# A layer-norm's statistics and its gate products moved between the bodies of a fused Mamba and MoE kernel

## The reference, cut to what matters

```python
x = x + tanh(g_xattn) * ssm(ctx, z=layernorm(x))        # ssm: conv, scan over 16 states, y * silu(z)
x = x + tanh(g_ffn)   * moe(layernorm(x))               # moe: softmax routing, 8 experts with adapters, shared expert

def _layernorm(x, axis=-1, eps=1e-05):
    m = jnp.mean(x, axis=axis, keepdims=True)
    v = jnp.var(x, axis=axis, keepdims=True)
    return (x - m) / jnp.sqrt(v + eps)
# in the ssm: y = y * jax.nn.silu(z), z the layer norm of x
```

## Time and profile before

| what | value |
|---|---|
| median of three runs | 1623.14 us (1621.38 to 1624.61) |
| profiled execution, its own time | 1615.96 us |
| its span | 1614.1 us |
| TensorE busy | 1509.3 us (94%) |
| VectorE busy | 1160.2 us (72%) |
| GpSimd busy | 743.1 us (46%) |
| ScalarE busy | 659.8 us (41%) |
| granted TensorE clock, mean | 0.978 |

### The profile page before, as it was taken

How to read it: one execution, slowest core, us unless ns; L and a number is a source line. 1 busy time by engine, 2 the same in 40 slices (tenths; PEclk the granted TensorE clock), 3 DMA queues, 4 the chain that set the end, 5 groups by cost and what they waited for, 6 DMA issues and landing times.

```text
span 1614.1 us, 19148 instructions
## 1 busy us (share of the span) xinstructions
PE 1509.3 (94%) x6440; PEld 1146.2 (71%) x6440; DVE 1160.2 (72%) x1638; ACT 659.8 (41%) x1035; POOL 743.1 (46%) x536
## 2 busy tenths in 40 slices
PE   5678799988888899999999999999999999999999
PEld 3334377766666667778777777777777777887787
DVE  6899867988899867688888856888888653333333
ACT  6555345544454434543444345434444321211111
POOL 3589421887878702287777401676777000000000
PEclk9799899998999999999999999999999999999999
DMA  7799538698878873889789645899897458778882
GB/s 257 260 334 313 208 114 273 212 317 291 280 269 286 282 257 143 246 294 296 249 254 276 230 150 200 261 301 276 265 283 231 172 191 261 223 220 247 252 244 97
DMA packets 144945, 395.99 MB, mean 245 GB/s; under 512 B 25456, under 2 KB 66672, under 8 KB 129616
## 3 DMA queue, kind: packets, MB, share of 16 engines
q1 hardware_dynamic: 124624, 342.07, 63.5%
q10 hardware_dynamic: 20224, 52.70, 11.3%
HBM read 306.30 MB, written 68.16 MB: 232 GB/s over the span
## 4 chain that ended last, share of the span: by engine, by line
PE 59%; DVE 17%; POOL 9%; issue 5%; ACT 5%; DMA 4%; ACTq 1%; SPq 1%; DVEq 0%; POOLq 0%
PE b_u L819 14%; PE b_g L819 14%; PE b_u L913 8%; POOL ring L1516 5%; PE b_q L913 4%; PE b_q L867 3%; DVE ring L1613 3%; PE b_g L913 3%; PE b_g L885 3%; DVE tt L1587 2%; DMA raw<-in_gu 2%; PE b_g L852 2%; PE b_u L852 2%; DVE ring L1619 2%; POOL gm L1461 2%
## 5 line engine op out<-in xcount | busy, mean ns | idle before, releaser
L1516 POOL TENSOR_TENSOR ring<-du,rep 128x512 f32<-128x512 f32 x256 | 348.5, 1369 | 136.8 <-DVE du L1695 106.3
L819 PE MATMUL b_g<-xnb,gm 128*128 128x512 f32 (+1 forms) x1440 | 352.6, 394 | 0.9 <-DVE xnb L1590 0.9
L819 PE MATMUL b_u<-xnb,gm 128*128 128x512 f32 (+1 forms) x1440 | 349.4, 392 | 0.8 <-DVE xx L1587 0.8
L1525 POOL TENSOR_TENSOR yx<-yx,ring 128x512 f32<-128x512 f32 x192 | 266.2, 1387 | 152.1 <-DVE ring L1619 151.5
L1613 DVE TENSOR_TENSOR_SCAN ring<-b_a,ring 128x512 f32<-128x512 f32 x256 | 310.8, 1214 | 16.0 <-ACT b_a L1060 14.3
L819 PEld LDWEIGHTS b_g<-xnb,gm 128*128 128x128 f32 (+1 forms) x1440 | 256.0, 179 | 78.9 <-issue 8.8
L819 PEld LDWEIGHTS b_u<-xnb,gm 128*128 128x128 f32 (+1 forms) x1440 | 257.4, 179 | 73.1 <-DVE xx L1587 2.0
L1587 DVE SCALAR_TENSOR_TENSOR tt<-tt,b_g 128x512 f32<-128x512 f32 (+1 forms) x120 | 82.0, 684 | 197.4 <-ACT tt L1060 197.2
L1060 ACT ACTIVATE b_a<-delta,cs 128x512 f32<-128x512 f32 x256 | 173.3, 681 | 80.0 <-DVE ring L1613 75.8
L913 PE MATMUL b_u<-dwt,hhl 128*128 128x512 f32 (+1 forms) x720 | 193.7, 399 | 3.0 <-DVE daw_s L1590 1.7
L1060 ACT ACTIVATE tt<-b_g 128x512 f32<-128x512 f32 (+1 forms) x120 | 71.2, 593 | 284.4 <-PE b_u L852 241.2
(11 more groups left out here) (248 smaller groups left out, 1923.9 us busy)
## 6 DMA issues: line engine op xcount, KB each, us to landing
gm<-scr_gm SPq DMA_DIRECT2D x64, 1024.0 KB, 9.3
dwt<-scr_dw SPq DMA_DIRECT2D x32, 1536.0 KB, 6.7
rep<-bc_d ACTq DMA_DIRECT2D x64, 512.0 KB, 7.0
gm<-scr_gm SPq DMA_DIRECT2D x32, 768.0 KB, 5.4
scr_gm<-gm SPq DMA_DIRECT2D x20, 1024.0 KB, 7.2
dqt<-scr_dq SPq DMA_DIRECT2D x25, 640.0 KB, 9.1
qat<-scr_qa SPq DMA_DIRECT2D x25, 512.0 KB, 9.2
awt<-aw_h ACTq DMA_DIRECT2D x48, 256.0 KB, 4.7
```

Source lines behind the costliest of these rows:

```text
L819: i = mm(out_b[0:IW[m], :], w, v, start=(n == 0), stop=(n == 11 and not is_routed(s)))
L1516: v.tensor_tensor(ring_at(nb, T), du[:, T % 4, :], rep[:, N % NREP, 0], ALU.mult).then_inc(pool_dbu, 1)
L1525: v.tensor_tensor(yd, yd, ring[:, T % NRING], ALU.add).then_inc(pool_y, 1)
```

## The change

On ScalarE the root moves from slot "b" of body 3 to its end, behind slot "f". On VectorE the row sums and the variances move to the end of body 3, behind slot "f" too, and the scales to body 4, in front of slot "b". The four tanh and gate products, two each in bodies 4 and 5, become one in body 4, two in body 5, and one in body 6. No instruction is added or taken away, and no transfer is touched.

```diff
@@ def tanh_z(nb, c), ScalarE
-                need(act, dve_daw, NF * (nb - 1) + (4 if c < 2 else 5))
+                need(act, dve_daw, NF * (nb - 1) + (4, 5, 5, 6)[c])
@@ def routed(b, e), ScalarE
                 slot("b")
                 if split_next:
                     hi("gm0", s + 1)
-                if more and e == 3:
-                    root(2 * nb)
                 if more and e == 4:
                     norm_z(nb, range(LC))
                     tanh_z(nb, 0)
                 if more and e == 5:
-                    tanh_z(nb, 2)
+                    tanh_z(nb, 1)
+                if more and e == 6:
+                    tanh_z(nb, 3)
                 tanh(s, 1)
                 slot("h1")
                 h_hi(s, 1)
-                if more and e == 4:
-                    tanh_z(nb, 1)
                 if more and e == 5:
-                    tanh_z(nb, 3)
+                    tanh_z(nb, 2)
...
                 slot("f")
+                if more and e == 3:
+                    root(2 * nb)
@@ def routed(b, e), VectorE
-                if more and e == 3:
-                    dve.wait_ge(dma_x, 16 * (nb + 1))
-                    for c in range(LC):
-                        row_sums(2 * nb, xx[nb % 2], c)
-                    variances(2 * nb)
+                if more and e == 4:
                     scales(2 * nb, True)
                 slot("b")
...
                 if more and e == 4:
                     gate_z(nb, 0)
                 if more and e == 5:
-                    gate_z(nb, 2)
+                    gate_z(nb, 1)
+                if more and e == 6:
+                    gate_z(nb, 3)
...
                 hidden(s, 1, mid("h1"))
                 slot("c")
-                if more and e == 4:
-                    gate_z(nb, 1)
                 if more and e == 5:
-                    gate_z(nb, 3)
+                    gate_z(nb, 2)
...
                 slot("f")
+                if more and e == 3:
+                    dve.wait_ge(dma_x, 16 * (nb + 1))
+                    for c in range(LC):
+                        row_sums(2 * nb, xx[nb % 2], c)
+                    variances(2 * nb)
```

## The result

The changed kernel takes 1627.36 us (median of 20 runs, 1624.15 to 1632.67), the kernel before 1621.20 (20 runs on the same chips, 1615.03 to 1624.61). The ratio is 1.0042, 95% interval [1.0031, 1.0053]: slower by 6 to 7 us (6.2 between the medians), where -0.5 was forecast, with -4 and +4 as bounds.

The account below looks back on a forecast made before the run. TensorE was taken to bound passes 1 and 2, VectorE pass 0. Pass 0 at -1.3 us and passes 1 and 2 together at +0.8 summed to -0.5: median 1622.6 us, range -4 to +4.

Parts of the forecast that it names:

- the term of the scales: Body 4: six instructions, 1.2 us, delay the normalizations 1.64 us; +0.9 us in each of passes 1 and 2, +0.6 in pass 0.
- The 0.7 that a gate product fewer gives back: Body 4: gate product 1 leaves, giving back about 0.7 us of the delay behind the scales.
- The block at the end of body 3: Seam to body 4: of 3.1 us of statistics 1.95 come to light; body 3 35.45 us, -0.5 in passes 1 and 2 each.
- Rival 2: End of body 3: the statistics are hidden whole, faster, total -7 us, 1616; chance 0.18, in part or whole.
- Pass 0: Body 3: third hidden tile begins by 418.8, body 4 1.9 us earlier (bounds -3.2 and 0); with scales +0.6, sum -1.3 us.
- TensorE's wait at the seam: Pass 0, end of body 3: TensorE waits some 2.6 us for VectorE's first addition in body 4.
- Rival 1: Seams before body 4: TensorE's clock falls behind the wait, 1.3 to 1.7 us each, total +4, 1627; chance 0.20, body 4's upper bound included.
- Root: ScalarE, behind the last exponential of body 3: cost 0; uncovered, 1.3 us a table load.
- gate: Body 5 holds two products as before, body 6 gets one of 0.68 to 2.47 us: cost 0; uncovered, up to 1.1 in pass 0.
- rival 3: Only moved: body 3's lateness reappears whole, half at the seam, half in body 4; no difference, 1623.1; chance 0.17.
- one of the prediction's signs of being wrong: A body 6 that grew; others were a seam without a wait, or a clock under 1.00 behind it in passes 1 and 2.

Follow-up runs that it names:

- with GpSimd held: The changed kernel, with GpSimd's step behind the first hidden tile of body 4 waiting until the next batch's scales are done: 1622.81 us, ratio to before 1.0016.
- The double block: The changed kernel with scales at the head of body 4 and the four row sums at the end of body 3 done twice: 1631.12 us, ratio to before 1.0058.
- spread version: The changed kernel with scales at the head of body 4 and row sums spread over bodies 2 and 3 (pass 0: within body 3): 1611.11 us, ratio to before 0.9943.
- the version with the scales at the head: The changed kernel with the six scale instructions moved to the head of body 4, behind the last down-projection's addition: 1618.99 us, ratio to before 0.9991.
- the spread version with the old gate: Scales at the head of body 4, row sums spread, gate products as before the change, two each in bodies 4 and 5: 1612.22 us, ratio to before 0.9946.

## Why the prediction was wrong

**The step that failed is the term of the scales: six instructions, 1.2 us.** At their new place they took 2.63 us in pass 1 and 4.22 in pass 0. The duration came from the earlier trace rows, where the six stand in body 3 of the kernel before. There GpSimd was quiet, because the long block of statistics just in front of them had left it without work (4.04 us idle, ended by VectorE's next product into the ring):

```profile
788.73 1.09 POOL L1525 TENSOR_TENSOR yx<-yx,ring 128x512 f32<-128x512 f32 x1 [4.04 <-DVE ring L1619]
```

At the new place a scan and the product behind it stand just in front of them, and that product is what gives GpSimd its next instruction (it ends its idle time at 820.53). So a price was read in one neighbourhood and used in another. The normalizations were forecast 1.64 us late against the body's start and were 3.23 late (10.94 us behind it, before 7.71). The rest of that step was sound: with GpSimd held, they are 1.77 late and body 4 costs 0.86 and 0.92 us more, where +0.9 was forecast. The 0.7 that a gate product fewer gives back was measured as 0.67. The prediction gives gate product 3 up to 2.47 us "when POOL works beside it", and did not ask the same of the scales. The trace of the kernel before even had one small instruction of the statistics that was held, in body 3 of pass 0: it took 0.70 us instead of 0.17 and ended 0.02 us after GpSimd's instruction. VectorE's row, then GpSimd's:

```profile
409.00 0.70 DVE L1635 TENSOR_SCALAR st<-mv 128x4 f32<-128x4 f32 x1
```

```profile
407.28 2.40 POOL L1461 TENSOR_TENSOR gm<-raw,gm 128x1024 fp32r<-128x1024 f32 x1
```

**The block at the end of body 3:** right in kind, too dear. It is one wait on the first addition, but of 1.00 and 0.92 us, not 1.95, so body 3 took 34.64 and 34.56, not 35.45. The slack was taken from the seams of bodies 2 and 4. In body 2 the last scan waits 1.02 us for ScalarE's exponential (the row at 774.02) and starts 4.04 us before the next body; in body 3 it waits 0.17 and starts 4.64 before TensorE is ready (807.06 to 811.70). So body 3 had at least 0.6 us more slack than its neighbours showed. Rival 2, hidden whole, would have given 33.49, further off.

**Pass 0:** Body 3 was forecast 1.9 us shorter and was 0.47 shorter (43.79 against 44.26). Its third hidden tile began 24.1 us behind the body's start, which is the later end of the forecast (418.8 - 394.61 = 24.2). From there to the first addition it took 18.87 us instead of 14.9 + 3.1 = 18.0, and the difference is the scales' error once more: the last small instruction of the block, beside GpSimd at the new place, took 1.01 us, where the price read in pass 1 has 0.17, and ended 0.03 us after GpSimd's. The other 0.6 us is that the forecast was set ahead of its own later end (-1.9 instead of -1.3). VectorE's row, then GpSimd's:

```profile
433.86 1.01 DVE L1635 TENSOR_SCALAR st<-mv 128x4 f32<-128x4 f32 x1
```

```profile
433.58 1.26 POOL L1516 TENSOR_TENSOR ring<-du,rep 128x512 f32<-128x512 f32 x1
```

TensorE's wait at the seam was forecast at 2.6 us and measured at 2.81. What was put at nothing is the clock behind it: the first twelve products took 4.62 us instead of the 3.04 of the earlier trace rows. Rival 1 is right in pass 0, at about 1.6 us, and did not happen in passes 1 and 2, where the wait was half of what it assumed. The double block shows it there behind waits of 3.44 and 3.50 us; what a wait of about 2 us, as forecast, would have done there, no run shows. Most of the loss of body 4 in pass 0, though, is the scales again: 2.5 of 4.66 us came back by moving them.

**Root, gate, rival 3:** the root cost nothing visible; the table loads behind it end before the first tanh has its products. The gate cost nothing that the time shows. But body 6 of pass 0, forecast unchanged, took 42.01 us instead of 40.26, which was one of the prediction's signs of being wrong. At a granted clock of 1.00 in both it took 40.84 with the gate product (spread version) and 40.26 without (kernel before), so the product is not wholly hidden there, by some 0.6 us; the rest of the growth goes with a lower clock (0.96). Rival 3, "only moved", described body 4 well (three waits, like the old body 3's), but the loss there is larger than what left body 3, for the reason above.

The sum, term by term, in passes 1 and 2 together: body 3 forecast at -1.0, measured -2.7; body 4 forecast at +1.8, measured +6.15. Bodies 3 and 4 of pass 0: forecast -1.3, measured +4.19. Most of the error in body 4 is the same in all passes, the held scales; in pass 0 the clock adds about 1.6 us.

## What to carry to other kernels

A duration is the price of an instruction beside its neighbours: before a small instruction is moved, look at what GpSimd does at the new place, and for each small one that it can hold count on what is left of GpSimd's instruction (here 0.5 to 2.2 us). A blocked instruction shows as a long one, not as idle time, so compare the durations of the same small instruction between places, and its end with the other engine's ends. Work off the bound engine is free when it is cut to the size of the waits that its engine already has (0.6 to 1.2 us pieces here), and dear as one block in front of something that the bound engine needs.

## What the runs showed of the hardware that was not expected

**Four elements can take 2.33 us.** `TENSOR_TENSOR` and `TENSOR_SCALAR` on VectorE, 0.16 to 0.17 us alone, took 0.70, 0.85, 0.94, 1.01, 1.05 and 2.33 us beside a GpSimd instruction, always ending 0.02 to 0.04 us after it. The two `RECIPROCAL` took 0.16 to 0.18 everywhere, also beside one (822.25, beside GpSimd's of 822.08). The Trainium skill, SBUF — State Buffer, section "SBUF: two separate sides", says that VectorE and GpSimd share a pair of ports as an exclusive lock, held for a whole instruction by whichever starts first: a GpSimd instruction, or a VectorE instruction that has two inputs in SBUF or runs in a mode that uses both ports. By that rule the victim's own size does not matter, and the trace agrees: the delay is what is left of GpSimd's instruction.

**The clock does not go by the length of one wait alone.** At the seam in front of body 4, the first twelve products kept full speed (the 2.4 GHz level) behind waits of 0.91 to 1.47 us in every trace (3.01 to 3.06 us), and lost it behind 2.47, 2.55, 2.81, 2.84, 3.44, 3.50 and 5.52 us (4.49 to 5.49). Inside body 6 of pass 0 the same wait went both ways. TensorE's timeline of the spread version, and then of the version with the scales at the head:

```profile
549.28 0.96 PE L885 MATMUL b_g<-hhl,dqt 96*128 96x512 f32 x3 [3.03 <-DVE hhl L1590]
550.08 1.55 PE L913 MATMUL b_q<-dwt,hhl 128*128 128x512 f32 x6
```

```profile
553.78 1.65 PE L885 MATMUL b_g<-hhl,dqt 96*128 96x512 f32 x3 [3.03 <-DVE hhl L1590]
555.22 2.76 PE L913 MATMUL b_q<-dwt,hhl 128*128 128x512 f32 x6
```

Behind 3.03 us of waiting the next six products took 1.55 us in one execution and 2.76 in the other; over body 6 the granted clock was 1.00 and 0.92. Much of the spread of body 6 comes from this: it took between 40.26 and 43.39 us over all the traces, with the gate product in it (40.84 to 43.39) and without (40.26 to 41.54). Whether that product makes the fall more likely there stays open: without it, too, the six products behind a wait of 2.30 us took 2.45 us instead of 1.61 in one trace (the spread version with the old gate); and the times of the two spread versions (1611.11 and 1612.22) don't show it.
